# Self attention's value products taken for two steps at once, in four column groups of TensorE

## The reference

```
h = _rms(x, w_ln1)
q = (h @ wq + bq).reshape(B, S, 16, 16)      # 16 heads of width 16
k = (h @ wk + bk).reshape(B, S, 16, 16)
v = (h @ wv + bv).reshape(B, S, 16, 16)
q, k = _rope(q, k)
scores = einsum('bqhd,bkhd->bhqk', q, k) * 16 ** (-0.5)
scores = where(causal, scores, finfo.min)
attn = softmax(scores, axis=-1)
ctx = einsum('bhqk,bkhd->bqhd', attn, v).reshape(B, S, 256)
x = x + ctx @ wo
```

## Time and profile before

| what | us |
|---|---|
| median of 3 runs | 1309.33 (1308.08 to 1310.52) |
| the profiled execution's own time | 1310.3 |
| its span | 1308.5 |
| TensorE busy in the span | 1217.0 (93%) |
| VectorE busy | 878.1 (67%) |
| ScalarE busy | 505.6 (39%) |
| the stretch of the self attention, 787 to 886 | 99.0 |

### The profile page before, as it was taken

How to read it: one execution, slowest core, us unless ns; L and a number is a source line. 1 busy time by engine, 2 the same in 40 slices (tenths; PEclk the granted TensorE clock), 3 DMA queues, 4 the chain that set the end, 5 groups by cost and what they waited for, 6 DMA issues and landing times.

```text
span 1308.5 us, 21984 instructions
## 1 busy us (share of the span) xinstructions
PE 1217.0 (93%) x8541; PEld 790.2 (60%) x8541; DVE 878.1 (67%) x1717; ACT 505.6 (39%) x1133; POOL 372.8 (28%) x385
## 2 busy tenths in 40 slices
PE   6889999999799999999999879998999898999997
PEld 4664658999546565665657545664556565456655
DVE  3776776677376666667667596777766757766666
ACT  3422460111133433433443225652443343555553
POOL 1510115565203333334113320000333333133332
PEclk9899999999899999999999997999999979999999
DMA  4030141000144444444410000000443200233342
GB/s 143 2 153 17 51 141 37 1 1 1 46 174 113 123 124 121 113 113 122 151 58 1 17 1 1 2 2 15 128 122 123 96 17 2 86 115 113 114 133 82
DMA packets 41544, 97.20 MB, mean 74 GB/s; under 512 B 5446, under 2 KB 18246, under 8 KB 39392
## 3 DMA queue, kind: packets, MB, share of 16 engines
q1 hardware_dynamic: 41440, 95.79, 23.8%
HBM read 94.35 MB, written 1.42 MB: 73 GB/s over the span
## 4 chain that ended last, share of the span: by engine, by line
PE 78%; DVE 13%; ACT 3%; issue 3%; POOL 2%; DMA 1%; SPq 0%; DVEq 0%; POOLq 0%; ACTq 0%
PE PS L1401 10%; PE PS L1402 10%; PE PS L1403 10%; PE PS L1446 5%; PE PS L1448 4%; PE PS L1447 4%; PE PS L1036 3%; PE PS L1054 2%; PE PS L1220 2%; PE PS L2050 2%; PE PS L2067 2%; PE PS L1022 2%; PE PS L1024 2%; PE PS L1023 2%; PE PS L2032 1%
## 5 line engine op out<-in xcount | busy, mean ns | idle before, releaser
L1616 POOL TENSOR_TENSOR arena<-arena,m_g 128x512 f32<-128x512 f32 x142 | 183.1, 1291 | 409.9 <-DMA m_g<-gate_rows 240.3
L1401 PE MATMUL PS<-arena 128*128 128x512 f16 x608 | 230.8, 380 | 4.7 <-DVE arena L1632 1.8
L1402 PE MATMUL PS<-arena 128*128 128x512 f16 x608 | 230.8, 380 | 0.0
L1403 PE MATMUL PS<-arena 128*128 128x512 f16 x608 | 230.7, 379 | 0.0
L1446 PE MATMUL PS<-arena 128*128 128x256 f16 x608 | 165.9, 273 | 9.5 <-DVE arena L1573 8.7
L1448 PE MATMUL PS<-arena 128*128 128x256 f16 x608 | 165.7, 273 | 0.0
L1447 PE MATMUL PS<-arena 128*128 128x256 f16 x608 | 165.7, 273 | 0.0
L1513 ACT ACTIVATE arena<-PS 128x512 f32<-128x512 f32 x112 | 66.9, 597 | 245.9 <-PE PS L1403 235.5
L1556 DVE SCALAR_TENSOR_TENSOR arena<-arena,PS 128x512 f32<-128x512 f32 x112 | 77.0, 688 | 124.1 <-ACT arena L1513 123.9
L1573 DVE TENSOR_TENSOR arena<-arena 128x512 f16<-128x512 f32 x142 | 112.0, 789 | 3.9 <-ACT arena L1523 3.9
L1403 PEld LDWEIGHTS PS<-arena 128*128 128x128 f16 x608 | 59.5, 98 | 71.9 <-issue 0.3
(11 more groups left out here) (282 smaller groups left out, 2301.2 us busy)
## 6 DMA issues: line engine op xcount, KB each, us to landing
w_stage<-in_up SPq DMA_DIRECT2D x80, 256.0 KB, 2.9
m_g<-gate_rows SPq DMA_DIRECT2D x70, 256.0 KB, 4.2
arena<-in_heads SPq DMA_DIRECT2D x16, 1088.0 KB, 6.5
w_stage<-in_down SPq DMA_DIRECT2D x80, 128.0 KB, 4.1
m_g<-gate_rows SPq DMA_DIRECT2D x17, 512.0 KB, 4.0
m_g<-gate_rows SPq DMA_DIRECT2D x6, 448.0 KB, 4.6
m_g<-gate_rows SPq DMA_DIRECT2D x6, 384.0 KB, 4.1
m_g<-gate_rows SPq DMA_DIRECT2D x6, 320.0 KB, 4.0
```

The costliest lines, as they stand in the source:

```text
L1401: pe.matmul(to, w_hi, x_hi, start=(k == 0), stop=False)
L1402: pe.matmul(to, w_lo, x_hi, start=False, stop=False)
L1403: ins = pe.matmul(to, w_hi, x_lo, start=False, stop=(k == KT - 1))
L1616: pool.tensor_tensor(m_c[:, st % 2, :], m_b[:, st % LAG, :], m_g[:, st // 2 % 2, st % 2, :], ALU.mult).then_inc(s.c, 1)
```

## The change

The values of two steps are taken together, in every even step from t = 2 on: `values(t - 2)` now covers steps t - 2 and t - 1, runs over the four pairs of heads j0 to j0 + 3 in its innermost loop, and so visits all four column groups in turn. It waits for both copies. `s.pv` is raised by 2 for each call. The turned probabilities get four slots where there were two: the slots of `sa_pt` and two more, `more_pt`, behind `sa_p`. `turned_part(t)` gives the slot of a step. The copy of step t waits for the values of step t - 4 and before. The products, their operands and their number stay.

```diff
+        more_pt, at = take(at, [2, 2, 512])
+        assert at <= 39424
...
+        def turned_part(t):
+
+            return (sa_pt, more_pt)[t % 4 // 2][:, t % 2, :, :]
...
             def values(t):
+
                 b, q, j0, keys = sa_part(t)
                 bq = t // SA_OF_Q
-                pe.wait_ge(s.pt, t + 1)
+                pe.wait_ge(s.pt, t + 2)
                 if j0 == 0:
                     pe.wait_ge(s.v, b + 1)
                     if bq >= 2:
                         pe.wait_ge(s.x2, bq - 1)
                 for a in range(2):
                     for k in range(q + 1):
-                        for e in range(2):
-                            j = j0 + e
+                        for j in range(j0, j0 + 4):
                             out_ps = PS[32 * (j % 4):32 * (j % 4) + 32, 6 + q, (j // 4) * P:(j // 4 + 1) * P]
                             ins = pe.matmul(out_ps, sa_vm[b][:, k, j, a, :, :].rearrange("p e c -> p (e c)"),
-                                            sa_pt[:, t % 2, e, (a * (q + 1) + k) * P:(a * (q + 1) + k + 1) * P],
+                                            turned_part(t + (j - j0) // 2)[:, j % 2, (a * (q + 1) + k) * P:(a * (q + 1) + k + 1) * P],
                                             start=(a == 0 and k == 0), stop=(a == 1 and k == q))
-                ins.then_inc(s.pv, 1)
+                ins.then_inc(s.pv, 2)
...
-                if t:
-                    values(t - 1)
+                if t and t % 2 == 0:
+                    values(t - 2)
...
-            values(SA_STEPS - 1)
+            values(SA_STEPS - 2)
             sums_transposed(B * QT - 1)
             project(B * QT - 1)
...
                 dve.wait_ge(s.pt_ps, t + 1)
-                if t >= 2:
-                    dve.wait_ge(s.pv, t - 1)
-                dve.tensor_copy(sa_pt[:, t % 2, :, 0:cols], PS[:, 2:4, 0:cols]).then_inc(s.pt, 1)
+                if t >= 4:
+                    dve.wait_ge(s.pv, t - 3)
+                dve.tensor_copy(turned_part(t)[:, :, 0:cols], PS[:, 2:4, 0:cols]).then_inc(s.pt, 1)
```

## The result

| | us |
|---|---|
| forecast | 1302.3 (1297.5 to 1307.5) |
| changed kernel, median of 20 runs | 1307.01 |
| kernel before, median of 20 runs | 1313.47 |
| ratio, after to before | 0.9957, interval 0.9940 to 0.9973 |
| span of the profiled execution, before and after | 1308.5 and 1305.2 |

The change makes the kernel faster by 0.43%, which is 5.6 of 1313.47, with 3.5 to 7.9 as its interval. The forecast was 7.0. Most of that, 4.1, is the kernel before: its three runs gave 1309.33, all its twenty 1313.47. Measured from 1313.47 the forecast of 1302.3 is a gain of 11.2, about twice the real one. The 7.0 itself lies inside the measured interval, so what is wrong with it only the traces can tell. One run of each kernel, 2074.97 before and 1576.69 after, was in a much slower state and is left out of the ratio.

A forecast was written before the change was run, and what follows sets the result against it. TensorE was taken as full in the self attention, with a loop through VectorE and ScalarE close behind. Gains 2.5 + 1.7 + 1.7 + 1.1 = 7.0 took 1310.3 to 1303.3, the median 1.0 lower: 1302.3, range 1297.5 to 1307.5.

The forecast's parts named there:

- The price of a call: Value products in self attention: a wide double call (32 instructions) costs 1.00, a narrow one (16) 0.56.
- Rival C: Value products: four groups don't run together while accumulating in PSUM, only shape changes are saved, 1308.5; chance 0.05.
- The narrow and wide blocks: Each period of eight steps: 0.4 gained at turned(20), 1.7 at turned(24), out of 3.6 saved on TensorE.
- the wait ahead of turned(18): Narrow block: TensorE waits 0.8 for the exp there, the saving of step 17 turned into a wait.
- Rivals A and B: Self attention: A, TensorE stays the bound, all 14.4 show, chance 0.10; B, loops are tighter, 3.2 gained, chance 0.16.
- the loop through exp: Wide block: transposes, copy, maxima and exp take 5.49 for two steps, a second bound 0.07 below TensorE's 5.56.
- rival D: Narrow blocks from step 8 on: waits bring back the low clock, 6.8 lost per block, three give 1322.7; chance 0.05.
- The last period: End of self attention: 0.4 at turned(31), then 0.7 behind it, 1.1 in all.
- The first period: First eight steps, partly at 1.2 GHz: 2.5 gained, bounds 1.7 to 3.5.
- the clock rises at a time and not at a step: First period: the low clock ends at 803.50 as before, so some of the 1.84 at turned(4) is given back.
- The starting point: Whole kernel before: its median stands 1.0 below the profiled execution of 1310.3.

The follow-up runs named there:

- one product: Changed kernel with only the first of the 2 or 4 rounds of value products per pair of heads; ratio to the kernel before 0.9933.
- evacuated later: Changed kernel with ScalarE's evacuation of the transposed sums one step later in its queue; ratio to the kernel before 0.9943.
- half the exps: Changed kernel with two of the four exps of each step left out; ratio to the kernel before 0.9871.
- scores first: Changed kernel with scores(t + 2) ahead of turned(t) on TensorE and maxima(t + 2) ahead of copy t on VectorE; ratio to the kernel before 0.9927.
- second trace: Changed kernel itself timed and traced once more, nothing altered; ratio to the kernel before 0.9965.
- warmed: Changed kernel with 8 warming products between the first two scores and the first transposes; ratio to the kernel before 0.9923.
- two groups: Changed kernel with a double call visiting two column groups at a time, not four; ratio to the kernel before 0.9981.

## Why the prediction was right or wrong

**The price of a call held.** 1.02 and 0.58 against 1.00 and 0.56; four groups do run together while they accumulate in PSUM. Rival C is out.

**The narrow and wide blocks held.** Per period the gain was 1.72 and 1.73 against 1.7. The single steps held too: turned(20) at 9.62 after turned(16) (844.93) for 9.6, turned(22) at 15.17 for 15.1, turned(23) at 18.17 for 18.1, the wait ahead of turned(18) 0.68 for 0.8. Rivals A and B are out. That only half of TensorE's saving comes through is shown from several sides: fewer products add nothing in the wide block and 0.65 in the narrow one (one product), and an earlier exp(18) adds its 0.57 there (evacuated later). In the wide block turned(22) waits for exp(22), and two steps from turned(20) on take 5.55, where the loop was put at 5.49. That the loop through exp holds it is shown by this wait; that it stands alone is not so, since the copy takes over within 0.3 of the block's time (half the exps, scores first). The prediction did not price that further bound, and for its own sum it did not matter. One reading of it was off without effect: 842.14 is the end of exp(18), turned(18) starts at 842.19, and the narrow step in rival D is 2.23 and not 2.28.

**The last period held.** 0.34 at turned(31) and 0.66 behind it, against 0.4 and 0.7.

**The first period failed.** It is the first of two steps that failed, and the one in the mechanism. It was put at 2.5, with 1.7 as its lower bound; it gave 1.08 and, in the second trace, nothing. The step that failed is "the clock rises at a time and not at a step": I took that time, 803.5, from the trace of before, as if the change could not move it. With double calls the low stretch went on for 17.1 and 20.5, not 13.7, and the wide steps that moved up ran at 1.2 GHz, turned(5) to turned(6) among them. Single calls in this period alone restored 13.7. So it is shown, on one trace each, that after a fall 0.8 behind turned(0) the double calls of the first period keep the clock low for 3.4 longer. Over all traces without warming it was 13.7 in the three with single calls there and 17.1 or 20.5 in five with double ones; but scores first has double calls and 10.2, and half the exps has them and no fall. The moment of the fall may have its part in this: the same kernel had 17.1 after a fall behind turned(0) and 20.5 after one ahead of it; but one product had 20.5 after a fall 1.37 behind it. How much of the 20.5 is the moment and how much the change stays open, and by what measure the chip decides is not shown. Without the low stretch (warmed) the first period gains 1.55. Rival D had the right mechanism in the wrong place: the low level does not come back in the later narrow blocks, it stays longer in the first.

**Behind the stretch** some is lost and some won. From the last addition to x to the end it took 422.46 before, 424.14 in the profiled execution of the changed kernel and 421.98 in its second trace. In both traces of the changed kernel the clock falls for 3.4 shortly after the stretch (892.8 and 898.1 into the span), and the low stretch of the next layer, 17.1 before, is 10.2. The instructions there are the same at the same spacing, so only their moment has moved. I counted this in the range and not in the sum; what decides these falls was not tried.

**The starting point failed.** "The median stands 1.0 below that execution" rested on three runs. Twenty gave 1313.47, and this step is 4.1 of the 4.7 by which the forecast time is off. The mean clock of the changed kernel's runs goes with their times, if loosely: 1301.8 to 1302.0 at 0.983 in three runs, 1311.3 to 1311.6 at 0.971 in three, but one of 1301.78 at 0.978. I read the scatter of one and the same kernel, some 10 and more than the whole change, as low stretches that come or stay away; only the profiled executions show them, so this is not shown run by run.

**In sum:** 1.1 + 1.7 + 1.7 + 1.0 = 5.5 in the stretch of the first trace (7.0 forecast), 4.4 in the second, and 5.6 by the ratio. That 5.5 and 5.6 agree is in part luck, with 3.3 between the two profiled executions. That 1307.01 lies within the forecast range is luck as well: the range was laid around a starting point 4.1 too low.

## What to carry to other kernels

When the busiest engine is relieved, price the chain next in length first. Here one line of arithmetic, copy plus maxima plus exp plus transposes for two steps against two steps of TensorE, 5.49 against 5.56, together with the wait for exp(18), cut a saving of 3.6 to 1.7 per period. Do not take the moment of a clock rise over from the old trace when the work under the low clock changes; where TensorE waits for its first operand, eight spare products there brought 4.8 to 5.3 in the stretch, nearly as much as the change. And the smaller the effect, the more runs the baseline needs: here three runs were off by 4.1, with an effect of 5.6.

## What the runs showed of the hardware

TensorE seems not to start matmuls strictly in program order when they lie in different column groups. Two traces say so. The trace doesn't name an instruction's column group, so this is a reading of the starts.

The first is the kernel with two groups. In program order the 16 instructions of the first two pairs of heads come ahead of the 16 of the other two. Two start every 0.11, so in strict order no more than these 16 would have started 0.85 after the first. But 24 had started by then, and all 32 took 1.48 in place of 1.88:

```profile
836.05 1.10 PE L2074 MATMUL PS<-arena 128*32 128x128 f32 x24
```

This is the timeline to 836.90; to 836.50 there are eight. So the second half began about 0.48 after the first, ahead of the last instructions of the first half.

The second is the kernel before. Of the 16 instructions of one call, two start within 0.01 and the next two 0.13 later. If the two instructions of an fp32 product follow each other in the program, as one call writes them, they go to one column group, and the second product's first half starts ahead of the first product's second:

```profile
830.08 0.30 PE L2067 MATMUL PS<-arena 128*32 128x128 f32 x2
```

This is all that had started in the first 0.12 (timeline to 830.20); up to 830.30 there are four. The Trainium skill, "TensorE: Matmul & The Clock Gate", section The mechanism, says that matmuls start and end in program order; by this reading these rows do not agree with it for the start, and the measurement decides. On the ends they say nothing, since those are modelled.
